# All weight-transposing steps of a transformer layer emitted during attention, none inside the feed-forward's first pass

## The reference

```python
# x: (4, 4096, 1024), 16 heads of 64
def attn(x):                       # x already layer-normed
    kc = conv1d(x, Wconv, stride=3)                 # 3 taps
    k_tmp = concat([x[:, :1, :], kc], axis=1)       # 1366 keys
    q, k, v = x @ Wq.T, k_tmp @ Wk.T, k_tmp @ Wv.T
    scores = einsum('bhqd,bhkd->bhqk', q, k) * HD ** (-0.5) + mask * -1e9
    return softmax(scores) @ v  @ Wo.T + bo         # heads joined

def ffn(x):                        # D_IN 1024, D_HID 4096, ternary weights
    h = silu(x @ w1_w.T * w1_s) * (x @ w2_w.T * w2_s)
    h = gelu(h @ h1_w.T * h1_s)                     # 4096 x 4096
    h = gelu(h @ h2_w.T * h2_s)                     # 4096 x 4096
    return h @ w3_w.T * w3_s

x = x + layernorm(attn(layernorm(x)))
x = x + layernorm(ffn(layernorm(x)))
```

## Time and profile before

| | us |
|---|---|
| median of 2 runs | 6491.76 (6487.84 to 6495.69) |
| the profiled execution | 6490.09 |
| its span, first to last instruction of the slowest core | 6488.4 |
| spans of the eight cores | 6441.9 to 6488.4 |

### The profile page before, as it was taken

The page is one execution under the profiler, slowest core; times in us unless marked ns, Lnnn a source line. Parts: engine busy times, 40 slices in busy tenths (PEclk is TensorE's granted clock), DMA queues, the critical chain, the costliest instruction groups (busy, mean ns, idle before and its releaser), DMA issues.

```text
span 6488.4 us, 39375 instructions; the slowest of 8 cores (6441.9 to 6488.4 us)
## 1 busy us (share of the span) xinstructions
PE 3298.7 (51%) x15168; PEld 1467.3 (23%) x15168; DVE 716.5 (11%) x1430; ACT 667.0 (10%) x928; POOL 98.3 (2%) x192
## 2 busy tenths in 40 slices
PE   0000255534443000021249984699937799669994
PEld 0000012212222000000114431244413344224441
DVE  0044101132211000200001001020011100020001
ACT  0000000022332000000002000120001110011000
POOL 0000000000000000000000000000000000000000
PEclk9999977755555555565669996899968799889996
DMA  9723443286996978676347544275533555355553
GB/s 128 144 93 97 89 71 65 51 99 182 126 123 180 130 190 116 162 197 180 81 105 184 140 113 115 71 183 141 143 92 87 139 147 151 96 131 149 137 142 91
DMA packets 1383255, 821.63 MB, mean 127 GB/s; under 512 B 607760, under 2 KB 1339040, under 8 KB 1368736
## 3 DMA queue, kind: packets, MB, share of 16 engines
q1 hardware_dynamic: 1362656, 625.12, 39.5%
q0 software_dynamic: 20416, 194.00, 17.5%
HBM read 627.12 MB, written 245.37 MB: 134 GB/s over the span
## 4 chain that ended last, share of the span: by engine, by line
PE 45%; DMA 28%; another core or an unknown queue 11%; SPq 9%; issue 3%; DVE 3%; ACT 1%; POOL 0%; DVEq 0%; ACTq 0%; POOLq 0%
PE ps_f L1186 28%; DMA p2b<-n_h 6%; DMA wbuf<-t_w 5%; DMA t_h<-p2b 4%; PE ps_f L1248 4%; PE ps_f L1120 4%; PE ps_f L1125 3%; PE ps_cv L462 3%; DMA p2b<-n_w 3%; SPq L904 2%; DMA t_w<-p2b 2%; DMA lx<-x_full 2%; DMA cv_nat<-wconv 2%; SPq L450 1%
## 5 line engine op out<-in xcount | busy, mean ns | idle before, releaser
L1186 PE MATMUL ps_f<-hslab,wbuf 128*128 128x512 bf16 x4096 | 913.1, 387 | 42.0 <-DMA wbuf<-t_h 42.0
L1186 PE MATMUL ps_f<-cslab,wbuf 128*128 128x512 bf16 x4096 | 891.4, 381 | 44.9 <-DMA wbuf<-t_h 44.9
L1120 PE MATMUL ps_f<-x2fm,wbuf 128*128 128x512 bf16 x1024 | 304.5, 451 | 917.9 <-DMA wbuf<-t_w 917.4
L462 PE MATMUL ps_cv<-xwin,wt_cv 128*128 128x512 bf16 (+1 forms) x576 | 183.1, 483 | 898.6 <-DMA wt_cv<-n_cv 898.6
L1186 PEld LDWEIGHTS ps_f<-hslab,wbuf 128*128 128x128 bf16 x4096 | 407.2, 99 | 547.9 <-issue 121.6
L1186 PEld LDWEIGHTS ps_f<-cslab,wbuf 128*128 128x128 bf16 x4096 | 402.1, 98 | 534.2 <-issue 55.6
L1248 PE MATMUL ps_f<-hslab,wbuf 128*128 128x512 bf16 x1024 | 258.5, 420 | 206.3 <-DMA wbuf<-t_w 206.3
L1120 PEld LDWEIGHTS ps_f<-x2fm,wbuf 128*128 128x128 bf16 x1024 | 109.4, 110 | 1086.0 <-issue 1009.4
L932 PE MATMUL ps_f<-ofm,wt_o 128*128 128x512 bf16 x256 | 61.6, 388 | 499.6 <-DMA ofm<-scr_o 499.4
L462 PEld LDWEIGHTS ps_cv<-xwin,wt_cv 128*128 128x128 bf16 x576 | 59.6, 105 | 1021.6 <-issue 1004.2
L1125 PE MATMUL ps_f<-x2fm,wbuf 128*128 128x512 bf16 x1024 | 265.2, 406 | 0.0
(11 more groups left out here) (83 smaller groups left out, 1807.9 us busy)
## 6 DMA issues: line engine op xcount, KB each, us to landing
wbuf<-t_h SPq DMA_DIRECT2D x256, 1024.0 KB, 9.3
n_h<-h POOLq DMA_DIRECT2D x32, 2048.0 KB, 100.1
t_h<-p2b POOLq DMA_DIRECT2D x64, 1024.0 KB, 4.2
wbuf<-t_w SPq DMA_DIRECT2D x128, 512.0 KB, 5.3
wbuf<-t_w SPq DMA_DIRECT2D x32, 1024.0 KB, 7.8
n_w<-w POOLq DMA_DIRECT2D x16, 1024.0 KB, 162.7
lx<-x_full SPq DMA_DIRECT2D x32, 512.0 KB, 3.7
t_w<-p2b POOLq DMA_DIRECT2D x16, 1024.0 KB, 4.2
```

Of the source, the lines that this page charges most:

```text
L462: ins = t.matmul(ps_cv[ot][:, 0:pn], wt_cv_t(kd)[:, ot * 128:(ot + 1) * 128], xwin_t(kd)[:, w:3 * (pn - 1) + w + 1:3], start=(w == 0 and k ...
L1120: t.matmul(pa[:, 0:TC], wbuf_t(par, kd)[:, mt * 128:(mt + 1) * 128], x2fm_t(kd), start=(kd == 0), stop=(kd == DT - 1))
L1186: ins = t.matmul(pb[mt][:, 0:TC], wbuf_t(par, k)[:, mt * 128:(mt + 1) * 128], src_t(k), start=(k == 0), stop=(k == DHT - 1))
```

## The change

The 64 steps of h2 and w3 join `p2_steps`, so that the eight pairs of attention emit 112 steps (16 each with pairs 0 to 6). The block loop of the w1/w2 pass in chunk 0 no longer emits casts or steps, nor does the place ahead of the h1 pass. Behind attention any casts left are emitted explicitly. The transposes of wo get a semaphore of their own, dWO.

```diff
--- before.py
+++ after.py
@@ -204,7 +204,7 @@
                   "dMK0", "dMK1", "dSO", "dOF0", "dOF1", "dAT0", "dAT1", "dTM0", "dTM1", "dTM2", "dTM3", "dL2", "dL3", "dLS2", "dLS3",
                   "dX2S0", "dX2S1", "dX2S2", "dX2S3", "dX2", "dFT2", "dFT3", "dLS0", "dLS1", "dY0", "dY1", "dPT0", "dPT1", "dPW0", "dPW1", "dW0", "dW1", "dFS", "dFT0", "dFT1", "dY", "dDG",
                   "dgA", "dgF", "dgH1", "dgH2", "dXP0", "dXP1", "dXP2", "dXP3",
-                  "dXL0", "dXL1", "cT", "cV", "cA"]:
+                  "dXL0", "dXL1", "dWO", "cT", "cV", "cA"]:
             sems[s] = stack.enter_context(nc.semaphore(s))
         blk = stack.enter_context(nc.Block())
         b = Bld(nc, blk, sems)
@@ -672,19 +672,13 @@
         for nat_, tdst_, I_, O_, gate_, mark_ in [
                 (n_w1, t_w1, D, DH, "dgF", None),
                 (n_w2, t_w2, D, DH, "dgF", "p2_ab"),
-                (n_h1, t_h1, DH, DH, "dgH1", "p2_h1")]:
+                (n_h1, t_h1, DH, DH, "dgH1", "p2_h1"),
+                (n_h2, t_h2, DH, DH, "dgH2", "p2_h2"),
+                (n_w3, t_w3, DH, D, "dgH2", "p2_w3")]:
             nkd = I_ // 128
             for kd_ in range(nkd):
                 p2_steps.append((nat_, tdst_, O_, gate_, kd_,
                                  mark_ if kd_ == nkd - 1 else None))
-        p2_steps_B = []
-        for nat_, tdst_, I_, O_, gate_, mark_ in [
-                (n_h2, t_h2, DH, DH, "dgH2", "p2_h2"),
-                (n_w3, t_w3, DH, D, "dgH2", "p2_w3")]:
-            nkd = I_ // 128
-            for kd_ in range(nkd):
-                p2_steps_B.append((nat_, tdst_, O_, gate_, kd_,
-                                   mark_ if kd_ == nkd - 1 else None))
         p2_i = [0]
 
         def emit_p2(nsteps):
@@ -853,6 +847,7 @@
                     for j in (2 * jp, 2 * jp + 1):
                         inc(sy.dma_start(scr_o[j * 128:(j + 1) * 128, :], otm_t(j)), "dSO")
                 bb.sync(_so)
+            emit_casts(10 ** 6)
             emit_p2(len(p2_steps))
             ev["otm"] = cnt["cV"]
             ev["scr_o"] = cnt["dSO"]
@@ -902,8 +897,8 @@
                     wait(sy, "cV", ev["otm"])
                     for kd in range(DT):
                         inc(sy.dma_start(wt_o_t(kd), n_wo[:, kd * 128:(kd + 1) * 128],
-                                         transpose=True), "dWK")
-                    ev["woT"] = cnt["dWK"]
+                                         transpose=True), "dWO")
+                    ev["woT"] = cnt["dWO"]
                 bb.sync(_w)
 
             def a3_ofl(g):
@@ -926,7 +921,7 @@
                         wait(t, "cV", ev["otm"])
                         wait(t, "cA", ev["attn_A"])
                     wait(t, "dOF0", ev[f"ofl{g}"])
-                    wait(t, "dWK", ev["woT"])
+                    wait(t, "dWO", ev["woT"])
                     wait(t, "cA", ev.get(f"at_ev{m % 2}", 0))
                     for kd in range(DT):
                         ins = t.matmul(ps_w[m % 2][:, 0:512],
@@ -1078,15 +1073,9 @@
                     ev["x2fm"] = cnt["dX2"]
                 bb.sync(_x2l)
 
-                if C == 0:
-                    p2_steps[:] = p2_steps_B
-                    p2_i[0] = 0
                 prev_T_ab = cnt["cT"]
                 for mb in range(DH // 256):
                     par = mb % 2
-                    if C == 0:
-                        emit_casts(4)
-                        emit_p2(4)
 
                     def _wl(sy, mb=mb, par=par, C=C, prev_T_ab=prev_T_ab):
                         if C == 0 and mb == 0:
@@ -1203,9 +1192,6 @@
                     ev[f"{dst_name}_all"] = cnt["cA"]
                     ev[f"{dst_name}_mm_done"] = cnt["cT"]
 
-                if C == 0:
-                    emit_casts(10 ** 6)
-                    emit_p2(10 ** 6)
                 _hid_pass(t_h1, h_t, c_t, SH1C, "c", ("cV", ev["h_all"]), "p2_h1")
                 _hid_pass(t_h2, c_t, h_t, SH2C, "d", ("cA", ev["c_all"]), "p2_h2")
```

## The result

| | us |
|---|---|
| median of the changed kernel | 6548.28 (22 runs) |
| median of the kernel before, beside it | 6519.53 (21 runs) |
| ratio | 1.006, 95% interval 1.003 to 1.009 |
| the profiled execution, span of its slowest core | 6526.8 (cores 6483.7 to 6526.8) |

The change makes the kernel slower by 0.6%, less than the 2% that were called the same.

A forecast was written before the change was run, and what follows sets the result against it. Serial transpose steps on SP's queue and one buffer were taken to bound chunk 0's w1/w2 pass and outlast attention; 6490 + 549 - 484 gave 6555 us, +1.0%, range 6515 to 6620.

The forecast's parts named there:

- the cover that the steps lose: Chunk 0's w1/w2 pass: some 65 us of w1/w2 and projection work ran beneath the 64 steps, afterwards paid openly.
- The 48 old steps outlast attention: End of attention: the old steps end 335 us after attention's matmuls, so any added behind them lie in the open.
- Cadences 11.2 and 6.1: Moved steps, strictly serial on one transpose buffer: 11.21 us per 4096-wide h2 step, 6.1 per 1024-wide w3 step.
- The cast wait is moved, not new: After the last seven casts: the wait of about 140 us passes from the wo load to the first h2 step.
- Casts to wo load end +549: From the last casts to the wo load's end: 701 us instead of 152.1, so the output projection comes 549 later.
- The pass -484: Chunk 0's w1/w2 pass, x2fm load to first h1 load: 234 us without steps instead of 718, 484 less.
- Sum +65: Whole kernel: +549 in the open less 484 in the pass gives 65 us more, 6555 us, +1.0%.
- The wo load is short in its new place: Deciding point of a rival, chance 0.05: a new cast wait keeps the wo load's transposes over 100 us; 6693 us.
- the 48th step ended at 2397 and not before 2000: Deciding point of a rival, chance 0.05: steps hide under attention, the 48th write before 2000; 6006 us.
- chunk 0's pass takes 232, not 130 us: Rival, chance 0.05: chunk 0's w1/w2 pass drops to chunk 3's 130 us, 104 less; 6451 us.
- a pass at the lower clock: Rival, chance 0.07: TensorE stays at the lower clock in chunk 0's w1/w2 pass, 117 us more; 6672 us.

The follow-up runs named there:

- the second pair: Both kernels, before and changed, traced again without any edit; ratios to before 1.0011 and 1.0084.
- before again: The kernel before, unchanged, traced a second time; ratio to before 1.0011.
- no late steps: The changed kernel with the 64 h2 and w3 steps left out and all casts kept; 6038.37 us, ratio to before 0.9254.
- first trace with two buffers: The changed kernel with a second transpose buffer during attention, w3 steps still in attention; ratio to before 0.991.
- last kernel: The changed kernel with two buffers, w3 steps in chunk 0's h2 pass, halved h2 steps behind its w1/w2 weight loads; 6238.19 us, ratio to before 0.96.

## Why the prediction was right

The forecast was +65 us, 6555 in all; the runs gave a median of 6548.28, and the mechanism, slower by the cover that the steps lose, is the one that the experiments show. That the two totals lie only 7 us apart is partly luck. The kernel before had a median of 6519.53 in the same runs and not the 6491.8 that the sum started from, so the medians differ by 29 us only, and the ratio gives about 39 us (20 to 58). It is the stages that carry the forecast. By its steps:

- *The 48 old steps outlast attention, so more steps lie in the open.* Right. The first projection matmul waited 1040 us (below) instead of 499, and the 48th step's write comes just ahead of the last casts as in the earlier trace rows.
- *Cadences 11.2 and 6.1.* 11.1 and 6.2: (2883.14 - 2538.78) / 31 and (3085.08 - 2891.69) / 31. 3 us less than put in for h2 and 4 more for w3, over 31 intervals each.
- *The cast wait is moved, not new.* Right: the first h2 write comes 141.7 us after the casts, forecast 147, and the wo load takes 11.67. The kernel without late steps, where it takes 154 again, and the wait at 2107 in the earlier trace rows show that it is the casts.
- *Casts to wo load end +549.* +543 in the first pair of traces, +546.5 in the second.
- *The pass -484.* -483.5 and -486.7.
- *Sum +65.* +60 in both pairs of traces. The ratio of the first runs, 1.006, lies lower than that (60 of 6466 is 0.9%, the upper end of its interval) and the one beside the second pair, 1.0084, near it; their intervals overlap.

The rivals fell as their deciding points said. The wo load is short in its new place, the 48th step ended at 2397 and not before 2000, and chunk 0's pass takes 232, not 130 us. As for a pass at the lower clock, here is TensorE's timeline at its start:

```profile
3107.99 11.70 PE L927 MATMUL ps_f<-ofm,wt_o 128*128 128x512 bf16 x40 [1040.26 <-DMA ofm<-scr_o]
...
3198.02 3.57 PE L1109 MATMUL ps_f<-x2fm,wbuf 128*128 128x512 bf16 x8 [72.53 <-DMA wbuf<-t_w]
3201.38 2.52 PE L1114 MATMUL ps_f<-x2fm,wbuf 128*128 128x512 bf16 x8
3203.74 1.89 PE L1109 MATMUL ps_f<-x2fm,wbuf 128*128 128x512 bf16 x8
3205.46 1.89 PE L1114 MATMUL ps_f<-x2fm,wbuf 128*128 128x512 bf16 x8
```

Eight matmuls from start to start in 3.36 us, and two groups later in 1.72: the 1.2 and then the 2.4 GHz level, after 72.53 us of idling and, before that, 1040. The mean granted clock of the pass is 0.79, chunk 1's was 0.80 in the earlier trace rows. The Trainium skill (TensorE: Matmul & The Clock Gate, Part 1) has half rate after idling and full rate again under steady work; this trace agrees. The Trainium skill (DMA: Bandwidth & Descriptors, Queues, rings and completion order) has each DMA engine take turns between the queues; that does not describe what transposes behind seven casts meet here, 148 and 154 us, where no semaphore makes them wait for these casts.

What the prediction did not see is how little of the move costs anything: it had the 60 us as work beneath 64 steps, but the cover comes once per block. Half of the steps could leave for nothing, and the cover is lost when the last ones leave.

## What to carry to other kernels

Work that is serial by its own chain costs its full length wherever it stands with nothing beside it; before hoisting it into an earlier phase, look whether that phase's queue is done before its compute is, for here it outlasted the compute by 335 us. To know what a woven step costs, compare count times its cadence alone with what the stage gains when the steps are gone; the difference, here 60 us, is all the cover there is. Then look per block: here each block covered about 4 us whether it had two steps or four, so half of the steps used up all of it. Where the serial chain is the limit, break the chain first (a second buffer took the cadence from 11.1 to 9.3 and from 6.2 to 3.9 us) and weave after that: of h2's steps, put behind the loads of the pass, 105 us were covered with two buffers, where all 64 late steps, ahead of the loads, had 60 covered with one. Read the gain on the slowest core: of 138 us in the stages, about 65 reached the kernel's time.

## What the runs showed of the hardware

- The eight DMA transposes of the wo load, issued by SP right behind seven DRAM-to-DRAM casts of GpSimd, held SP's queue for 138 to 154 us in the three traces with one buffer that have them there (before, before again, no late steps; all cores), with the DMA engines' share at 1.00 to 1.01. In the last kernel, with two buffers, they held it for 95 to 122. With no casts ahead they take 11.3 to 13.9 us in the two traces of the changed kernel.
- A write of 256 KB out of the transpose buffer, 2.3 us to landing as a median in the trace of before, held the next transpose for 7 us when 2 MB of weight loads were issued just before it.
- With two buffers, 4096-wide steps went at 9.3 us each with the DMA engines at 0.85; 1024-wide ones at 3.9.
- On core 1 of the first trace with two buffers, a stretch with a granted clock of 0.77 instead of 0.87 took 960 us instead of 860.
